# One mixer-and-experts kernel on one core: the last front unit in halves, dense weights loaded in pieces, two loads moved ahead of a store

## The chip, the core and the metric

The kernel runs on one core of a Trainium2 chip. A core has TensorE (PE, matrix products into PSUM), VectorE (DVE), ScalarE (ACT), GpSimd (POOL) and SyncE (SP), whose queue issues all DMAs here; 16 DMA engines carry them. Each engine runs its own list of instructions in order and waits on semaphores. The metric is the time of one execution in microseconds (us).

## The reference, cut to what matters

Batch B = 4, length L = 1024. A selective state-space layer over `ctx`, gated by the layer norm of `x`, then a dense layer with 8 low-rank experts, top 2 of them per token:

```python
x = einsum('ed,bld->bel', in_proj_w, ctx)             # 1024 channels from 512
u = silu(causal_conv4(x) + conv_b)                    # taps t, t-1, t-2, t-3
dt_lo, Bm, Cm = split(einsum('ke,bel->bkl', x_proj_w, u))   # 32, 16, 16 rows
delta = softplus(dt_proj_w @ dt_lo + dt_proj_b)
state = state * exp(delta * A) + (delta * u) * Bm     # 16 states a channel, over l
y = (sum_n state_n * Cm_n + D * u) * silu(layernorm(x))
x = x + y
x = x + layernorm(x) @ W_base.T + b_base + top2_experts(layernorm(x))
```

## The kernel before, in words

**Tiling.** Channels lie on the 128 partitions and time along the free dimension. A *unit* U = 8 b + c is 128 channels (c = 0 to 7) of batch b. There are 32 *blocks* E, one for each unit's scan, with 16 *steps* each, one for each state n. Step m of block E on VectorE is `scan` (L1055) over 128x1024 elements. The term that it adds is `du * B_n`: for 10 or 11 of the steps VectorE makes it (`drive`, L1040) from a row of B that TensorE spread over the partitions into PSUM (`spread`, L483). For the steps in `B_ROWS` (1, 3, 6, 8, 11, 14) GpSimd makes it (`drive_rows`, L1187) from `b_rows`, which a DMA spreads. GpSimd multiplies each scan's result with `c_rows` (`product`, L1194), and TensorE adds the 16 products up in `y_ps` (`add_up`, L489). `gated_y` (L1062) makes `yy` of it on VectorE at step 2 of the next block.

**Front.** Before block E can run, its batch needs projection, convolution, SiLU (this gives `u`, stored to `u_d`), and the reduction by `w_x`, which gives `xd`: the 16 B rows, the 16 C rows and the 32 `dt` rows. For batches 1 to 3 this lies between the steps of earlier blocks. For batch 0 it stands alone ahead of block 0: for c = 0 to 7 TensorE projects into `row[c % 2]` (`project_first`), ScalarE begins the convolution (`begin_first`), VectorE adds three taps (`taps_first`), ScalarE applies SiLU (`finish_u`), TensorE reduces into `y_ps` (`reduce_first`). Then ScalarE copies `xd` in two halves (`take_xd`), VectorE splits it into three bf16 parts in six instructions, and TensorE makes `dt` (L590) and the first spread.

**SP's queue.** It stores each `u` and loads the next projection weights; after the last unit it loads the context of batch 1, `skip` (u of unit 0 read back, which GpSimd multiplies with `delta` to `du` in `make_du`), stores the B and C rows to `bc_d`, and, when that has landed, loads `b_rows` and `c_rows` from it. Of `c_rows` there is a ring of 4 places: the load for product q waits for product q - 4. Then follow the dense layer's weights `w_ra` (288 KB) and `w_o` (4 MB); the dense layer starts in block 9.

**Blocks 9 to 31** hold the dense layer for one tile of 128 tokens each beside the scans, and the tiles that are left run after the last scan.

Of the kernel before, what the change touches and what calls it, by code (L numbers as in the profile page):

```python
# [88 lines left out]
def program(nc, t_in, out):  # L89
# [5 lines left out]
    with ExitStack() as stack:  # L95
# [77 lines left out]
        first_begun, first_step, first_done, conv_first = (sem(n) for n in ("first_begun", "first_step", "first_done", "conv_first"))  # L173
        split_high, split_rest, split_mid, split_rest2, split_done = (sem(n) for n in (
# [44 lines left out]
        def _(sp):  # L219
# [110 lines left out]
            for c in range(NE):  # L330
                load_w_in(c + 2)
                store_u(c)
            for k in range(NK):
                load_ctx(1, k)
            load_u_again(0)
# [8 lines left out]
            sp.dma_start(w_ra[:, :, :], t_in["w_ra"]).then_inc(dense_in, 16)  # L344
            sp.dma_start(w_o[:, :, :], t_in["w_o"]).then_inc(dense_in, 16)

            def section(E, m):
# [3 lines left out]
                if last:  # L351
                    if m == 4:
                        store_bc(b + 1)
                    for i, n in enumerate(B_ROWS):
                        if m == max(n + 1, 6 + i):
                            load_b(b + 1, i)
                if m == 2 and j >= 1:
                    store_half(j - 1, 1)
# [53 lines left out]
        def _(pe):  # L412
# [157 lines left out]

            def reduce_first(c):

                pe.wait_ge(u_ready, c + 1)
                for h in range(2):
                    last = nc.tensor.matmul(y_ps[:, half(h)], w_x[:, c, :], decay[:, c % DECAYS, half(h)], start=(c == 0), stop=(c == NE - 1),
                                            skip_group_check=True)
                last.then_inc(u_used, 1)
# [4 lines left out]
            for c in range(2, NE):  # L582
                project_first(c)
                reduce_first(c - 2)
            reduce_first(NE - 2)
            reduce_first(NE - 1)
# [9 lines left out]
            def section(E, m):  # L596
# [19 lines left out]
                if dense and m == 4:  # L616
                    if j == 0:
                        pe.wait_ge(dense_in, 32)
# [57 lines left out]
        def _(act):  # L676
# [51 lines left out]
            def soften(E):  # L728
# [4 lines left out]
                else:  # L733
                    act.wait_ge(dt_ready, 2)
                    nc.scalar.activation(delta[:, 0, :], row[0][:, :], ACT.Softplus, bias=ch[:, 0, NC + 1:NC + 2]).then_inc(delta_ready, 1)
# [27 lines left out]
            def take_xd(b, h):  # L763

                if b == 0:
                    act.wait_ge(u_used, NE)
# [114 lines left out]

            table(LOGEXP)
# [11 lines left out]
            for c in range(NE):  # L894
# [3 lines left out]
                if c == 1:  # L898
                    gate_rows(0)
            table(SOFT)  # L900
# [101 lines left out]
        def _(dve):  # L1002
# [13 lines left out]

            def taps(E, i):
# [87 lines left out]
            for c in range(NE):  # L1105
                taps_first(c)

# [174 lines left out]
```

## Time and profile before

| | us |
|---|---|
| median of 3 runs (lowest, highest) | 2097.69 (2096.14, 2099.48) |
| profiled execution, its own time | 2104.84 |
| its span | 2103.0 |

| engine | busy us | share of the span |
|---|---|---|
| TensorE (PE) | 1782.0 | 85% |
| VectorE (DVE) | 1787.7 | 85% |
| GpSimd (POOL) | 1767.9 | 84% |
| ScalarE (ACT) | 1256.7 | 60% |

The profile is of one execution. Its rows give for an instruction, or a run of like ones, the start and duration, the engine, the line of the kernel, the operation, and its output and inputs. In brackets stands the idle time of the engine just before it, with what ended it.
### The profile page before, as it was taken

Reading aid. Unit: us, or ns where it says so; the run is one execution under the profiler, and the core shown is the slowest. Engines: PE = TensorE matmul, PEld = TensorE weight load, DVE = VectorE, ACT = ScalarE, POOL = GpSimd, SP = SyncE. Lnnn points to the kernel's source line nnn. Section 1 sums busy time; section 2 is a strip of 40 time slices with the busy share of each in tenths; the row PEclk is TensorE's granted clock in tenths of the full one; section 3 lists DMA queues with packets and bytes.
Section 4 is the critical chain, followed back from the end, with each engine's and each line's share of the span. In section 5 each row is a group of like instructions: output and inputs, shape, how many; then the busy total and the mean of one; then the engine's idle time right before and its main releaser. Section 6 shows DMA issues by size and latency. Waiting matters only on the chain.

```text
span 2103.0 us, 23735 instructions
## 1 busy us (share of the span) xinstructions
PE 1782.0 (85%) x7996; PEld 1094.4 (52%) x7996; DVE 1787.7 (85%) x1432; ACT 1256.7 (60%) x1701; POOL 1767.9 (84%) x796
## 2 busy tenths in 40 slices
PE   8767777877788899889989899899888888888999
PEld 3344554545455555555655555555555555555554
DVE  3589999999899999998989999988989999997111
ACT  3346655555666766766666666766666666663431
POOL 0279999999999999999989999999999999997200
PEclk9788778778779999999989999999999999989999
DMA  4565555576756666697755566686665666565200
GB/s 153 216 251 186 200 198 193 196 244 234 281 197 197 228 217 214 216 320 257 245 194 192 213 217 210 207 310 243 237 206 199 212 200 215 196 214 214 108 30 30
DMA packets 157977, 435.88 MB, mean 207 GB/s; under 512 B 14528, under 2 KB 47552, under 8 KB 157728
## 3 DMA queue, kind: packets, MB, share of 16 engines
q1 hardware_dynamic: 157856, 434.37, 60.2%
q8 instruction: 63, 1.03, 0.2%
q14 instruction: 58, 0.48, 0.1%
HBM read 383.46 MB, written 50.86 MB: 207 GB/s over the span
## 4 chain that ended last, share of the span: by engine, by line
DVE 39%; PE 29%; issue 17%; POOL 7%; ACT 5%; DMA 3%; DVEq 0%; SPq 0%; POOLq 0%; ACTq 0%
DVE state L1055 23%; DVE row L1040 10%; PE bank_a L545 8%; PE y_ps L489 6%; POOL prod L1194 5%; DVE conv L1032 3%; PE bank_b L545 3%; PE row L567 3%; PE row L483 2%; PE bank_b L449 2%; PE bank_a L556 1%; ACT decay L809 1%; PE bank_b L440 1%; POOL drive_rows L1187 1%; DMA xrow<-in_x 1%
## 5 line engine op out<-in xcount | busy, mean ns | idle before, releaser
L1194 POOL TENSOR_TENSOR prod<-state,c_rows 128x1024 f32<-128x1024 f32 x512 | 1200.3, 2359 | 91.8 <-DVE state L1055 40.3
L1055 DVE TENSOR_TENSOR_SCAN state<-decay,row 128x1024 f32<-128x1024 f32 x334 | 762.8, 2284 | 7.4
L489 PEld LDWEIGHTS y_ps<-ident,prod 128*128 128x128 f32 x4096 | 520.2, 152 | 296.2 <-issue 189.8
L489 PE MATMUL y_ps<-ident,prod 128*128 128x128 f32 x4096 | 592.5, 294 | 44.2 <-POOL prod L1194 41.2
L1040 DVE TENSOR_TENSOR row<-du,row 128x1024 f32<-128x1024 f32 x334 | 404.3, 1210 | 41.6 <-PE row L483 37.7
L809 ACT ACTIVATE row<-delta,a 128x1024 f32<-128x1024 f32 x178 | 199.0, 1118 | 379.9 <-DVE state L1055 379.0
L1187 POOL TENSOR_TENSOR drive_rows<-du,b_rows 128x1024 f32<-128x1024 f32 x178 | 420.9, 2365 | 1.9 <-DMA b_rows<-bc_d 1.9
L1055 DVE TENSOR_TENSOR_SCAN state<-row,drive_rows 128x1024 f32<-128x1024 f32 x178 | 404.7, 2274 | 17.9 <-POOL drive_rows L1187 16.8
L545 PE MATMUL bank_a<-w_o,xnT 128*128 128x512 f32 x816 | 402.0, 625 | 18.1 <-DVE x L1102 18.1
L809 ACT ACTIVATE decay<-delta,a 128x1024 f32<-128x1024 f32 x334 | 374.1, 1135 | 0.0
L483 PE MATMUL row<-parts,sel 96*128 96x512 bf16 x668 | 223.6, 419 | 173.9 <-DVE state L1055 171.6
L545 PEld LDWEIGHTS bank_a<-w_o,xnT 128*128 128x128 f32 x816 | 158.2, 201 | 168.6 <-issue 134.2
L483 PEld LDWEIGHTS row<-parts,sel 96*128 96x128 bf16 x668 | 56.6, 103 | 213.1 <-DVE state L1055 204.3
L1177 POOL TENSOR_TENSOR du<-delta,skip 128x1024 f32<-128x1024 f32 x32 | 75.4, 2356 | 88.5 <-DMA skip<-u_d 88.5
L440 PE MATMUL bank_b<-ctx,w_in 128*128 128x512 f32 x288 | 137.5, 609 | 0.0
L678 ACT ACT_TABLE_LOAD x97 | 124.5, 1283 | 2.4 <-PEq L1273 0.7
L685 ACT ACTIVATE xrow<-xrow 128x1024 f32<-128x1024 f32 x32 | 33.7, 1053 | 114.9 <-DMA xrow<-in_x 114.9
L459 PE MATMUL bank_b<-ident,xrow 128*128 128x128 f32 x256 | 48.3, 320 | 46.0 <-ACT delta L725 40.7
L449 PE MATMUL bank_b<-xd,w_bdt 32*128 32x512 f32 x124 | 86.6, 784 | 0.0
L556 PE MATMUL bank_a<-w_bdt,gT 65*128 65x512 f32 x110 | 63.2, 658 | 25.2 <-ACT gT L870 25.2
L1032 DVE SCALAR_TENSOR_TENSOR conv<-bank_b,ch,conv 128x512 f32<-128x512 f32 (+3 forms) x108 | 80.9, 749 | 3.3
L440 PEld LDWEIGHTS bank_b<-ctx,w_in 128*128 128x128 f32 x288 | 54.4, 196 | 50.8 <-issue 47.4
(131 smaller groups left out, 1636.8 us busy)
## 6 DMA issues: line engine op xcount, KB each, us to landing
c_rows<-bc_d SPq DMA_DIRECT2D x512, 512.0 KB, 4.4
xrow<-in_x SPq DMA_DIRECT2D x32, 512.0 KB, 7.1
skip<-u_d SPq DMA_DIRECT2D x32, 512.0 KB, 6.0
yy_d<-yy SPq DMA_DIRECT2D x32, 512.0 KB, 6.3
b_rows<-bc_d SPq DMA_DIRECT2D x24, 512.0 KB, 8.5
u_d<-conv SPq DMA_DIRECT2D x24, 512.0 KB, 5.3
ctx<-u_d SPq DMA_DIRECT2D x48, 256.0 KB, 5.8
x<-in_x SPq DMA_DIRECT2D x24, 512.0 KB, 5.9
```

The source lines that it names most:

```text
L440: last = nc.tensor.matmul(bank[:, :], w_in[:, U % 2, k, :], ctx[:, k, half(h)], start=(k == 0), stop=(k == NK - 1))
L449: nc.tensor.matmul(bank_b[:, :], w_bdt[96:96 + DR, E % NE * P:(E % NE + 1) * P], xd[96:96 + DR, half(h)], start=True, stop=True).then_inc( ...
L483: last = nc.tensor.matmul(row[n % 2][:, half(h)], sel[:, SPREAD.index(n), :], parts[:, E // NE % 2, half(h)], start=True, stop=True)
L489: last = nc.tensor.matmul(y_ps[:, i * P:(i + 1) * P], source[:, i * P:(i + 1) * P], ident[:, :], start=(first and i % (H // P) == 0), stop ...
L545: nc.tensor.matmul(at.sums[h][:, :], at.xnT[:, k, :], w_o[:, k, half(h)], start=(k == 0), stop=False)
L678: nc.scalar.preload_act_table_set(name)
L809: nc.scalar.activation(to[:, :], delta[:, E % 2, :], ACT.Exp, scale=a[:, E % NE, n:n + 1]).then_inc(decay_ready, 1)
L1032: nc.vector.scalar_tensor_tensor(to, bank[:, 0:end - h * H - back], ch[:, c, NC - 1 - back:NC - back], to, ALU.mult, ALU.add).then_inc(con ...
L1040: nc.vector.tensor_tensor(row[n % 2][:, :], du[:, E % 2, :], row[n % 2][:, :], ALU.mult).then_inc(dve_drive, 1)
L1055: nc.vector.tensor_tensor_scan(state[:, q % STATES, :], factor, term, 0.0, ALU.mult, ALU.add).then_inc(scan_done, 1)
L1187: nc.gpsimd.tensor_tensor(drive_rows[:, i % DRIVES, :], du[:, E % 2, :], b_rows[:, k, :], ALU.mult).then_inc(pool_drive, 1)
L1194: nc.gpsimd.tensor_tensor(prod[:, q % PRODS, :], state[:, q % STATES, :], c_rows[:, q % RING, :], ALU.mult).then_inc(prod_ready, 1)
```

## The change

Three things are changed.

*The last unit of batch 0's front (c = 7) runs in two halves of 512 columns.* `project_end` does all four k of half 0, then those of half 1, with a semaphore after each. `begin_end`, `taps_end`, `finish_end` and `reduce_end` work on a half each. `take_xd` of half 0 waits for half 0's reduction alone. The softplus of block 0 (`soften`) is in halves too, each behind its half of `dt`.

*The dense weights are loaded during block 1*: `w_ra` at step 0, and `w_o` in eight pieces of 512 KB at steps 3 to 10.

*`skip` for block 0 and the context of batch 1 are issued before the store of the last u.*

On TensorE, around the last unit (L567/L572/L583 projections, L575/L601/L594 reductions, L590/L620 `dt`), before:

```order
L567 MATMUL row<-ctx,w_in 128x512 x8
L575 MATMUL y_ps<-decay,w_x 128x512 x2
L567 MATMUL row<-ctx,w_in 128x512 x8
L575 MATMUL y_ps<-decay,w_x 128x512 x6
L590 MATMUL row<-xd,w_bdt 128x512 x2
L483 MATMUL row<-parts,sel 128x512 x2
```

and the same place in the change:

```order
L601 MATMUL y_ps<-decay,w_x 128x512 x2
L583 MATMUL row<-ctx,w_in 128x512 x8
L601 MATMUL y_ps<-decay,w_x 128x512 x4
L594 MATMUL y_ps<-decay,w_x 128x512 x2
L620 MATMUL row<-xd,w_bdt 128x512 x2
L488 MATMUL row<-parts,sel 128x512 x2
```

The count is the same; L583 goes half by half, and the last unit's two reductions are now L594, with a wait each.

On SP's queue, from the store of unit 6 to the loads of `b_rows` and the dense weights, before (L245 stores u, L226 context, L261 `skip`, L266 `bc_d`):

```order
L245 DMA u_d<-decay 128x1024
L235 DMA w_in<-in_w_in 128x512
L245 DMA u_d<-decay 128x1024
L226 DMA ctx<-in_ctx 128x1024 x4
L261 DMA skip<-u_d 128x1024
L266 DMA bc_d<-xd 32x1024
L282 DMA b_rows<-bc_d 128x1024
L275 DMA c_rows<-bc_d 128x1024
L282 DMA b_rows<-bc_d 128x1024
L275 DMA c_rows<-bc_d 128x1024 x2
L282 DMA b_rows<-bc_d 128x1024 x4
L344 DMA w_ra<-in_w_ra 128x576
L345 DMA w_o<-in_w_o 128x8192
```

and in the change:

```order
L247 DMA u_d<-decay 128x1024
L237 DMA w_in<-in_w_in 128x512
L263 DMA skip<-u_d 128x1024
L228 DMA ctx<-in_ctx 128x1024 x4
L247 DMA u_d<-decay 128x1024
L268 DMA bc_d<-xd 32x1024
L284 DMA b_rows<-bc_d 128x1024
L277 DMA c_rows<-bc_d 128x1024
L284 DMA b_rows<-bc_d 128x1024
L277 DMA c_rows<-bc_d 128x1024 x2
L284 DMA b_rows<-bc_d 128x1024 x4
L277 DMA c_rows<-bc_d 128x1024 x6
```

`skip` and the context stand ahead of the last u store, and `c_rows` follows `b_rows` directly.

On SP's queue in block 1, from step 0 on, in the change (L359 and L361 are the dense weights, L290 stores `yy`, L242 loads `xrow`):

```order
L359 DMA w_ra<-in_w_ra 128x576
L277 DMA c_rows<-bc_d 128x1024 x3
L361 DMA w_o<-in_w_o 128x1024
L290 DMA yy_d<-yy 128x8x128
L277 DMA c_rows<-bc_d 128x1024
L361 DMA w_o<-in_w_o 128x1024
L277 DMA c_rows<-bc_d 128x1024
L361 DMA w_o<-in_w_o 128x1024
L242 DMA xrow<-in_x 128x1024
L277 DMA c_rows<-bc_d 128x1024
L361 DMA w_o<-in_w_o 128x1024
```

One piece stands behind each `c_rows`; three more pairs like this follow, and `skip` and `w_in` between them.

```diff
--- before.py
+++ after.py
@@ -171,6 +171,8 @@
         x0_ready, x_ready, conv_begun, conv_step, conv_done, u_ready, u_used, us_used, xd_copied = (sem(n) for n in (
             "x0_ready", "x_ready", "conv_begun", "conv_step", "conv_done", "u_ready", "u_used", "us_used", "xd_copied"))
         first_begun, first_step, first_done, conv_first = (sem(n) for n in ("first_begun", "first_step", "first_done", "conv_first"))
+        end_begun, end_step, end_done, end_x, end_u, end_used = (sem(n) for n in (
+            "end_begun", "end_step", "end_done", "end_x", "end_u", "end_used"))
         split_high, split_rest, split_mid, split_rest2, split_done = (sem(n) for n in (
             "split_high", "split_rest", "split_mid", "split_rest2", "split_done"))
         first_split = sem("first_split")
@@ -329,10 +331,11 @@
             sp.dma_start(sel[:, :, :], t_in["pick"]).then_inc(sel_in, 16)
             for c in range(NE):
                 load_w_in(c + 2)
+                if c == NE - 1:
+                    load_u_again(0)
+                    for k in range(NK):
+                        load_ctx(1, k)
                 store_u(c)
-            for k in range(NK):
-                load_ctx(1, k)
-            load_u_again(0)
             store_bc(0)
             load_b(0, 0)
             load_c(0)
@@ -341,8 +344,6 @@
                 load_c(i)
             for i in range(2, len(B_ROWS)):
                 load_b(0, i)
-            sp.dma_start(w_ra[:, :, :], t_in["w_ra"]).then_inc(dense_in, 16)
-            sp.dma_start(w_o[:, :, :], t_in["w_o"]).then_inc(dense_in, 16)
 
             def section(E, m):
                 b, r, j = E // NE, E % NE, E - LATE
@@ -354,6 +355,10 @@
                     for i, n in enumerate(B_ROWS):
                         if m == max(n + 1, 6 + i):
                             load_b(b + 1, i)
+                if E == 1 and m == 0:
+                    sp.dma_start(w_ra[:, :, :], t_in["w_ra"]).then_inc(dense_in, 16)
+                if E == 1 and m in range(3, 3 + NE):
+                    sp.dma_start(w_o[:, m - 3, :], t_in["w_o"][:, m - 3, :]).then_inc(dense_in, 16)
                 if m == 2 and j >= 1:
                     store_half(j - 1, 1)
                 if m == 3:
@@ -568,11 +573,32 @@
                                                 start=(k == 0), stop=(k == NK - 1), skip_group_check=True)
                 last.then_inc(x0_ready, 1)
 
+            def project_end():
+
+                c = NE - 1
+                pe.wait_ge(first_done, c - 1)
+                pe.wait_ge(w_in_in[c % 2], 16 * (c // 2 + 1))
+                for h in range(2):
+                    for k in range(NK):
+                        last = nc.tensor.matmul(row[c % 2][:, half(h)], w_in[:, c % 2, k, :], ctx[:, k, half(h)],
+                                                start=(k == 0), stop=(k == NK - 1), skip_group_check=True)
+                    last.then_inc(x0_ready if h else end_x, 1)
+
+            def reduce_end(h):
+
+                c = NE - 1
+                if h == 0:
+                    pe.wait_ge(end_u, 1)
+                else:
+                    pe.wait_ge(u_ready, NE)
+                nc.tensor.matmul(y_ps[:, half(h)], w_x[:, c, :], decay[:, c % DECAYS, half(h)], start=False, stop=True,
+                                 skip_group_check=True).then_inc(u_used if h else end_used, 1)
+
             def reduce_first(c):
 
                 pe.wait_ge(u_ready, c + 1)
                 for h in range(2):
-                    last = nc.tensor.matmul(y_ps[:, half(h)], w_x[:, c, :], decay[:, c % DECAYS, half(h)], start=(c == 0), stop=(c == NE - 1),
+                    last = nc.tensor.matmul(y_ps[:, half(h)], w_x[:, c, :], decay[:, c % DECAYS, half(h)], start=(c == 0), stop=False,
                                             skip_group_check=True)
                 last.then_inc(u_used, 1)
 
@@ -580,10 +606,14 @@
             project_first(1)
             pe.wait_ge(w_x_in, 16)
             for c in range(2, NE):
-                project_first(c)
+                if c < NE - 1:
+                    project_first(c)
+                else:
+                    project_end()
                 reduce_first(c - 2)
             reduce_first(NE - 2)
-            reduce_first(NE - 1)
+            reduce_end(0)
+            reduce_end(1)
             pe.wait_ge(w_bdt_in, 16)
             for h in range(2):
                 pe.wait_ge(xd_copied, h + 1)
@@ -615,7 +645,7 @@
                     turn(j, m - 2, beside, True)
                 if dense and m == 4:
                     if j == 0:
-                        pe.wait_ge(dense_in, 32)
+                        pe.wait_ge(dense_in, 16 * (NE + 1))
                     route(j, beside)
 
                 for i, at in enumerate(front_plan(E)[0]):
@@ -731,8 +761,10 @@
                     act.wait_ge(v_copied, 2 * E)
                     nc.scalar.activation(delta[:, E % 2, :], delta[:, E % 2, :], ACT.Softplus).then_inc(delta_ready, 1)
                 else:
-                    act.wait_ge(dt_ready, 2)
-                    nc.scalar.activation(delta[:, 0, :], row[0][:, :], ACT.Softplus, bias=ch[:, 0, NC + 1:NC + 2]).then_inc(delta_ready, 1)
+                    for h in range(2):
+                        act.wait_ge(dt_ready, h + 1)
+                        last = nc.scalar.activation(delta[:, 0, half(h)], row[0][:, half(h)], ACT.Softplus, bias=ch[:, 0, NC + 1:NC + 2])
+                    last.then_inc(delta_ready, 1)
 
 
             def begin_conv(E, i):
@@ -763,7 +795,10 @@
             def take_xd(b, h):
 
                 if b == 0:
-                    act.wait_ge(u_used, NE)
+                    if h == 0:
+                        act.wait_ge(end_used, 1)
+                    else:
+                        act.wait_ge(u_used, NE)
                 else:
                     act.wait_ge(us_used, ((b - 1) * 2 + h + 1) * NE)
                     act.wait_ge(dt_ready, 2 * NE * b)
@@ -879,6 +914,24 @@
                 nc.scalar.activation(decay[:, c % DECAYS, :], row[c % 2][:, :], ACT.Identity, bias=ch[:, c, NC:NC + 1],
                                      scale=ch[:, c, NC - 1:NC]).then_inc(first_begun, 1)
 
+            def begin_end(h):
+
+                c = NE - 1
+                if h == 0:
+                    act.wait_ge(end_x, 1)
+                    act.wait_ge(u_used, c - DECAYS + 1)
+                    act.wait_ge(u_out[c % 2], 16 * ((c - DECAYS) // 2 + 1))
+                else:
+                    act.wait_ge(x0_ready, NE)
+                nc.scalar.activation(decay[:, c % DECAYS, half(h)], row[c % 2][:, half(h)], ACT.Identity, bias=ch[:, c, NC:NC + 1],
+                                     scale=ch[:, c, NC - 1:NC]).then_inc(end_begun, 1)
+
+            def finish_end(h):
+
+                act.wait_ge(end_done, h + 1)
+                u = decay[:, (NE - 1) % DECAYS, half(h)]
+                nc.scalar.activation(u, u, ACT.Silu).then_inc(u_ready if h else end_u, 1)
+
             table(LOGEXP)
             act.wait_ge(consts_set, 2)
             act.wait_ge(ch_in, 16)
@@ -891,12 +944,16 @@
             act.wait_ge(a_step, 1)
             nc.scalar.activation(a[:, :, 0:DS], a[:, :, 0:DS], ACT.Copy, scale=-1.0).then_inc(a_step, 1)
             table(SILU)
-            for c in range(NE):
+            for c in range(NE - 1):
                 if c:
                     begin_first(c)
                 finish_u(c)
                 if c == 1:
                     gate_rows(0)
+            for h in range(2):
+                begin_end(h)
+            for h in range(2):
+                finish_end(h)
             table(SOFT)
             for h in range(2):
                 take_xd(0, h)
@@ -1014,6 +1071,18 @@
                     nc.vector.scalar_tensor_tensor(decay[:, c % DECAYS, back:], row[c % 2][:, 0:L - back], ch[:, c, NC - 1 - back:NC - back],
                                                    decay[:, c % DECAYS, back:], ALU.mult, ALU.add).then_inc(first_step if back < NC - 1 else first_done, 1)
 
+            def taps_end(h):
+
+                c = NE - 1
+                dve.wait_ge(end_begun, h + 1)
+                for back in range(1, NC):
+                    if back > 1:
+                        dve.wait_ge(end_step, h * (NC - 2) + back - 1)
+                    first = H if h else back
+                    to = decay[:, c % DECAYS, first:half(h).stop]
+                    nc.vector.scalar_tensor_tensor(to, row[c % 2][:, first - back:half(h).stop - back], ch[:, c, NC - 1 - back:NC - back],
+                                                   to, ALU.mult, ALU.add).then_inc(end_step if back < NC - 1 else end_done, 1)
+
             def taps(E, i):
 
                 U, h = HALVES[E][i]
@@ -1102,8 +1171,10 @@
                 nc.vector.tensor_tensor(x, x, at.sums[h][:, :], ALU.add).then_inc(res_ready, 1)
 
             dve.wait_ge(ch_in, 16)
-            for c in range(NE):
+            for c in range(NE - 1):
                 taps_first(c)
+            for h in range(2):
+                taps_end(h)
 
 
             rest = state[0:96, 0, :]
```

## Rows read from the trace of the kernel before

**Rows 1.** Busy time by stretch: from:to, us, each engine's busy us, granted clock, DMA share, GB/s.

```profile
91.40:165.80 74.40, 49.76 (x197) 29.10 (x197) 60.93 (x41) 37.91 (x47) 59.93 (x26) 0.73 0.72 268
165.80:223.00 57.20, 42.78 (x192) 26.60 (x192) 54.98 (x38) 32.95 (x40) 53.59 (x24) 0.80 0.58 195
```

**Rows 2.** Timeline of VectorE: start, us, operation, idle before and releaser.

```profile
106.14 1.23 DVE L1040 TENSOR_TENSOR row<-du,row 128x1024 f32<-128x1024 f32 x1 [2.64 <-PE row L483]
...
122.02 2.29 DVE L1055 TENSOR_TENSOR_SCAN state<-row,drive_rows 128x1024 f32<-128x1024 f32 x1 [6.67 <-POOL drive_rows L1187]
...
128.96 2.29 DVE L1055 TENSOR_TENSOR_SCAN state<-row,drive_rows 128x1024 f32<-128x1024 f32 x1 [1.20 <-POOL drive_rows L1187]
...
165.75 1.22 DVE L1062 TENSOR_TENSOR yy<-gate,y_ps 128x1024 f32<-128x1024 f32 x1 [1.73 <-PE y_ps L489]
...
223.03 1.22 DVE L1062 TENSOR_TENSOR yy<-gate,y_ps 128x1024 f32<-128x1024 f32 x1 [1.73 <-PE y_ps L489]
```

**Rows 3.** Timeline of GpSimd, its fourth product.

```profile
117.35 2.34 POOL L1194 TENSOR_TENSOR prod<-state,c_rows 128x1024 f32<-128x1024 f32 x1 [12.55 <-DMA c_rows<-bc_d]
```

**Rows 4.** DMA issues: count, KB each, us to landing; b_rows: minimum, median, maximum.

```profile
w_o<-in_w_o SPq DMA_DIRECT2D x1, 4096.0 KB, 21.7
...
bc_d<-xd SPq DMA_DIRECT2D x1, 128.0 KB, 6.5
...
c_rows<-bc_d SPq DMA_DIRECT2D x1, 512.0 KB, 22.5
...
DMA to landing us min/median/max: 3.9/9.1/11.1
```

**Rows 5.** Timeline around the last unit of the front.

```profile
68.61 1.06 ACT L760 ACTIVATE decay<-decay 128x1024 f32<-128x1024 f32 x1 [3.98 <-DVE decay L1014]
...
71.80 3.60 PE L575 MATMUL y_ps<-decay,w_x 128*128 128x512 f32 x8
...
73.24 3.92 DVE L1014 SCALAR_TENSOR_TENSOR decay<-row,ch,decay 128x1023 f32<-128x1023 f32 x3 [4.67 <-ACT decay L879]
...
77.19 1.06 ACT L760 ACTIVATE decay<-decay 128x1024 f32<-128x1024 f32 x1 [3.98 <-DVE decay L1014]
...
78.30 3.19 PE L575 MATMUL y_ps<-decay,w_x 128*128 128x512 f32 x4 [2.90 <-ACT decay L760]
...
81.53 1.08 ACT L773 ACTIVATE xd<-y_ps 128x512 f32<-128x512 f32 x2 [1.98 <-PE y_ps L575]
...
86.06 1.11 ACT L735 ACTIVATE delta<-row,ch 128x1024 f32<-128x1024 f32 x1 [3.44 <-PE row L590]
```

**Rows 6.** Timeline at the start of block 0.

```profile
88.15 1.01 PE L483 MATMUL row<-parts,sel 96*128 96x512 bf16 x2 [2.13 <-DVE parts L1118]
...
88.98 2.35 POOL L1177 TENSOR_TENSOR du<-delta,skip 128x1024 f32<-128x1024 f32 x1 [88.54 <-DMA skip<-u_d]
...
91.36 1.23 DVE L1040 TENSOR_TENSOR row<-du,row 128x1024 f32<-128x1024 f32 x1 [3.36 <-POOL du L1177]
...
95.59 2.29 DVE L1055 TENSOR_TENSOR_SCAN state<-row,drive_rows 128x1024 f32<-128x1024 f32 x1 [0.67 <-POOL drive_rows L1187]
```

**Rows 7.** Groups by line and shape, 60 to 170 us: busy us, mean ns | idle before.

```profile
L1032 DVE SCALAR_TENSOR_TENSOR conv<-bank_a,ch,conv 128x512 f32<-128x512 f32 x6 | 4.5, 746 | 0.1
...
L750 ACT ACTIVATE conv<-bank_a,ch 128x512 f32<-128x512 f32 x2 | 1.5, 759 | 0.0
```

**Rows 8.** Timeline of SP's queue: issue of the DMAs.

```profile
72.00 0.33 SPq L235 DMA_DIRECT2D w_in<-in_w_in  x1
...
78.27 0.33 SPq L245 DMA_DIRECT2D u_d<-decay  x1
...
82.64 0.32 SPq L266 DMA_DIRECT2D bc_d<-xd  x1
```

**Rows 9.** Landings of c_rows issued from 150 to 215 us.

```profile
DMA to landing us min/median/max: 3.5/4.3/5.6
```

**Rows 10.** Busy time by stretch, columns as in rows 1.

```profile
94.80:106.00 11.20, 8.31 (x21) 4.22 (x22) 8.00 (x5) 4.40 (x5) 9.99 (x5) 0.50 1.05 398
```

## The prediction, as it was written before the changed kernel had run

> **What bounds the kernel now.** I read the page first, then the engines by stretch, then VectorE's timeline for its idle times, then GpSimd's timeline and the DMA landings for what ended them, and last the timeline from 64 to 96 us. In the steady part VectorE sets the pace: in block 1 (166 to 223 us) it is busy 54.98 of 57.20 us, GpSimd 53.59 [rows 1], and one block takes 57.28 us from one `yy` product to the next (165.75 to 223.03) [rows 2]. Neither has time to win back a loss, so what the start loses stays lost. Block 0 with its lead-in (91.4 to 165.8) is longer: VectorE is busy 60.93 of 74.40 us [rows 1]. Its idle pieces are 2.64 us behind a spread on TensorE, 6.67 and 1.20 us behind GpSimd's drive rows, and the 1.73 us before `yy` that block 1 has as well [rows 2]. GpSimd was late because its fourth product sat 12.55 us waiting for its `c_rows` [rows 3]. That load took 22.5 us to land where its like in block 1 takes 4.3; the DMA issued just ahead of it is `w_o`, 4 MB, 21.7 us [rows 4, 9]. Before block 0 lies a serial chain through the last unit (c = 7) of the front: projection, taps, SiLU, reduction, `xd`, the split, `bc_d`, `b_rows`, first drive row [rows 5, 6].
>
> **Part 1, the dense weights out of block 0.** This removes 4.3 MB from the queue between the six `b_rows` and the fourth `c_rows`. The 12.55 us wait goes, and I ask what is late next. The slowest `b_rows` needs 11.1 us [rows 4], and the last is issued at 93.3, so the queue ahead of the fourth `c_rows` is drained at 104.4. Another 0.5 MB at the 398 GB/s of that stretch [rows 10] is 1.3 us: it lands at 105.7. GpSimd is ready for it at 104.8 (117.35 less 12.55) [rows 3], so 0.9 us of wait is left. VectorE wants the drive row behind that product only after its convolution at 115.4 (122.02 less 6.67) [rows 2]. With product and drive row at 2.35 us each the drive row is ready at 105.7 + 4.7 = 110.4, 5 us early. The next one (for the scan that starts at 128.96 now) follows product 5, which can start when scan 5 ends at 113.1, and is ready at 113.1 + 4.7 = 117.8; VectorE wants it at 128.96 - 6.67 - 1.20 = 121.1. So both waits go: 6.67 + 1.20 = 7.9 us gained. Bounds: 5 if a third of it comes back as a late `c_rows`, and 7.9 + 2.6 = 10.5 if the wait behind TensorE goes too. That wait is a matter of the clock: from 94.8 to 106 the granted clock is 0.50 [rows 10], the 1.2 GHz level, and TensorE does a gate turn, a projection piece, an add-up and the spread one after the other. The cause, pauses of TensorE before, is still there, so I keep the 2.6 us of wait.
>
> The Trainium skill (TensorE: Matmul & The Clock Gate, "What's actually happening") says that the throttled clock is the default and activity releases it. The trace agrees in that TensorE falls to 0.50 after its 2.90 us pause before the last reduction [rows 5, 10]. By this rule a front with a shorter pause could keep 2.4 GHz for the matmuls behind it; my sum does not count on it.
>
> **Part 2, the dense weights into block 1.** Added there: `w_ra` (0.3 MB) at step 0 and eight 0.5 MB pieces of `w_o` at steps 3 to 10, one behind each `c_rows` on SP's queue; also queued there are `yy_d` at step 3, `xrow` at 5, `skip` and `w_in` at 7. 4.2 MB over eight steps of 57.28 / 16 = 3.6 us is 146 GB/s on top of 195 [rows 1], 341 together, under the 398 that the queue has done [rows 10]. A piece puts off its successor by 1.3 us. A `c_rows` is issued three products before its use, some 10 us, and lands in 4.3 (5.6 at most) [rows 9], so 4 us are spare. `xrow` may come 1.3 us late, and ScalarE has its idle pieces there. I take 0.3 us of loss, bounds 0 and 3. The 9-fold count that TensorE waits for before its first routing (block 9) has been reached for hundreds of us. SP issues ten DMAs where it issued two; each takes 0.3 to 0.5 us of a 3.6 us step, hidden in its waits for products.
>
> **Part 3, the last unit in halves.** Half 0 of the projection is done at 71.8 - 8 x 0.43 = 68.5 (0.43 is 3.60 us / 8 matmuls, rounded down for the overlap of the last). ScalarE is free at 69.7 [rows 5], and starts half 0 then. A half takes 0.76 on ScalarE, and 3 x 0.75 on VectorE [rows 7], where 1.20 and 3.92 stood for the whole. So: half 0 begun 69.7 to 70.5, taps to 72.8; half 1 begun 72.0 to 72.8 (the projection ends at 71.97), taps to 75.1; SiLU of half 1 to 75.7 (1.06 for a whole, 0.55 taken for a half), against 78.25. TensorE works at unit 5's and 6's reductions up to 75.4, then half 0's to 76.3 and half 1's to 77.2, at 0.43 a matmul since it no longer pauses. The table load (1.28, from 75.7) ends at 77.0, so the `xd` copies run 77.0 to 78.1 in place of 81.53 to 82.61 [rows 5]. Gain up to here 4.5 us. Extra work is 0.3 us on ScalarE and 0.6 on VectorE, counted in. From the end of `xd` to the spread are 88.15 - 82.61 = 5.54 us of splitting on VectorE, and the spread takes 1.0 [rows 6]: the first drive on VectorE can start at 84.7 instead of 91.36, and its scan ends at 84.7 + 1.24 + 2.29 = 88.2.
>
> **Part 4, u's first load and the context ahead of u's last store.** Today GpSimd's first product waits for `skip` until 88.98, though `delta` is ready at 87.2 [rows 5, 6]. Now `skip` is issued at 72.4 behind `w_in`, first in line, and is there long before `delta`: with softplus in halves `delta` is ready at 80.0 with the fast clock, 81.7 with the slow. `du` then ends by 84.1 at the latest, before the spread at 84.7, so it no longer decides. The next thing that does is the first drive row: `bc_d` is stored, lands, `b_rows` is loaded (3.9 us), GpSimd multiplies (2.35). Between 78.27 and 82.64 SP queued u 0.52, context 2.10, `skip` 0.52 and `bc_d` 0.13 MB, 3.27 together, and `bc_d` landed at 89.2, 6.5 us after its issue [rows 8, 4]: 10.9 us after the first issue. Now 3.54 MB (`w_in` is 0.26) are queued from 72.0 on; in proportion 11.8 us, so 83.8. Hence `b_rows` at 87.7, the drive row at 90.05, scan 1 at 90.1 where it now starts at 95.59 [rows 6]: **5.5 us gained**. If `bc_d` takes its 6.5 us again (78.15 + 6.5 = 84.7), it is 4.6. If it lands by 81.9, scan 0's end at 88.2 decides, and it is 7.4. I stay near the middle, since the proportion uses the same transfers. The last u store lands with that queue, at 83; only the third decay factor waits for it, made at 83.5 or later.
>
> The Trainium skill (DMA: Bandwidth & Descriptors, "Anatomy of one DMA") gives a fixed cost of about 2 us for one DMA, whatever its size. The 6.5 us of the 128 KB `bc_d` [rows 4] is over three times that, so here the queue ahead decides. By the rule's price `bc_d` would land near 80.4 and the front would gain 7.4 us; the total would be 15.0 instead of 13.1.
>
> **The sum.** 5.5 + 7.9 - 0.3 = 13.1 us. The profiled execution took 2104.84 us (span 2102.98), so it would take 2091.7. It lies 7.15 above the median of 2097.69; I take the same difference off the median: **2084.6 us**. Behind block 1 the order of all engines is unchanged; only the phase of the granted clock moves, for which I allow 2 us each way.
>
> **Rivals.**
> - *More than the sum.* TensorE's 2.6 us wait in block 0 goes as well, or `bc_d` is early (+1.9). For it: shorter pauses in the front. Against: the pause of the split remains. 2097.7 - 13.1 - 2.6 = 2082, with both 2080.
> - *The front gives little.* The context loads, now in front of the u store, hold `bc_d` up, and halves cost more than in the rows: gain 3 instead of 5.5, or less. For it: `bc_d` today lands only when the queue is empty. Against: this queue begins 6.3 us earlier. 2087 to 2090.
> - *The stall stays.* The six `b_rows` and not `w_o` held up `c_rows`. Then only the front's gain shows: 2092. Against: 104.4 is when the last `b_rows` lands, 12.9 us before the product starts.
> - *Slower than before.* In block 1 the pieces of `w_o`, with `yy_d`, `xrow` and `skip`, make each `c_rows` late, and GpSimd, with 3.6 us of idle in the block, passes on every wait. The spare is 4 us; for the change to come out slower by over 0.2% it would need 13.4 + 4.2 = 17.6 us of waits, 2.2 at each of eight products beyond the spare, so landings from some 12 us on where 4.3 are seen. The price from there: 2102. Against: 341 of 398 GB/s.
>
> **Chances.** Forecast 0.66; more than the sum 0.15; front gives little 0.10; the stall stays 0.05; slower 0.02; the rest, a drift of the clock's phase that gives back all, 0.02. 0.2% (4.2 us) is about what a measurement of this kernel can tell from no change, so faster begins below 2093.5: all of the first three and most of the fourth, 0.94; same 0.04; slower 0.02. For the range I take the forecast with its bounds, 2080 for the upper case, and up to 2090 for the front that gives little.
>
> **What would show it.** `xd` copied near 78.1, first scan near 86, second near 90; `skip` no longer GpSimd's releaser; no `c_rows` wait over 2 us in block 0, and the first `yy` at 165.75 - 13.4 = 152.4; block 1 at 57.3 to 57.6. A first `yy` later than 156, or a second one more than 60 us behind it, would make the prediction wrong.

## The result, and the profile after

| | before | changed |
|---|---|---|
| median of 13 runs, us (lowest to highest) | 2096.65 (2093.27 to 2100.5) | 2086.44 (2078.69 to 2093.05) |
| ratio, 95% interval | | 0.9948 (0.9934 to 0.9961) |
| profiled execution / span, us | 2104.84 / 2103.0 | 2086.44 / 2084.7 |

The change takes 10.9 us off by the ratio (8.2 to 13.8; the medians lie 10.2 apart), where 13.1 had been forecast; the median is 2086.44, forecast 2084.6. Every ratio here is against the kernel before as it ran beside that kernel, and of fast executions alone, which leaves out one of e9's eleven, at 3634.83 us. Two later sets of runs of the same kernel gave 0.9925 (0.9907 to 0.9944) and 0.9951 (0.9933 to 0.9968). The profiled execution of before took 4.3 us more than the longest of its 13 timed ones, so the 18.3 us between the two spans (2103.0 less 2084.7) overstate the gain.

VectorE's timeline of the changed kernel (start, us, operation, idle before) answers to [rows 2, 6]:

```profile
79.98 3.43 DVE L1189 CAST parts<-state 32x1024 bf16<-32x1024 f32 x2
...
86.65 1.23 DVE L1109 TENSOR_TENSOR row<-du,row 128x1024 f32<-128x1024 f32 x1 [1.27 <-PE row L488]
...
90.61 2.29 DVE L1124 TENSOR_TENSOR_SCAN state<-row,drive_rows 128x1024 f32<-128x1024 f32 x1 [0.41 <-POOL drive_rows L1258]
...
100.40 1.23 DVE L1109 TENSOR_TENSOR row<-du,row 128x1024 f32<-128x1024 f32 x1 [1.88 <-PE row L488]
...
151.94 1.22 DVE L1131 TENSOR_TENSOR yy<-gate,y_ps 128x1024 f32<-128x1024 f32 x1 [1.72 <-PE y_ps L494]
209.22 1.22 DVE L1131 TENSOR_TENSOR yy<-gate,y_ps 128x1024 f32<-128x1024 f32 x1 [1.72 <-PE y_ps L494]
```

Scan 1 starts at 90.61 instead of 95.59, and the first `yy` at 151.94 instead of 165.75: 13.8 us are won by then. (0.2 of them are not the change's: the front, up to where nothing was edited, ran that much earlier in this execution; see the column "unit 6" below.) No scan in block 0 waits for drive rows after scan 1. Block 1, with the dense weights in it, takes 57.28 us as before.

The wait behind TensorE is 1.88 us where it was 2.64. TensorE no longer pauses 2.90 us before the last reduction, and its granted clock (the figure behind the five engines' busy times) is low for a shorter time: 0.50 from 79 to 106 us before, and now

```profile
82.50:99.00 16.50, 9.29 (x17) 3.36 (x18) 14.21 (x9) 8.47 (x10) 11.13 (x6) 0.50 0.90 328
99.50:116.00 16.50, 13.43 (x77) 9.14 (x76) 15.42 (x11) 7.67 (x11) 14.93 (x8) 1.00 0.64 225
```

GpSimd's timeline has the fourth product's wait [rows 3] down to

```profile
88.24 2.34 POOL L1258 TENSOR_TENSOR drive_rows<-du,b_rows 128x1024 f32<-128x1024 f32 x1 [5.37 <-DMA b_rows<-bc_d]
...
100.36 2.36 POOL L1265 TENSOR_TENSOR prod<-state,c_rows 128x1024 f32<-128x1024 f32 x1 [0.54 <-DMA c_rows<-bc_d]
```

and the front's chain on ScalarE and SP's queue reads

```profile
69.33 0.76 ACT L926 ACTIVATE decay<-row,ch 128x512 f32<-128x512 f32 x1
71.77 0.78 ACT L926 ACTIVATE decay<-row,ch 128x512 f32<-128x512 f32 x1 [1.67 <-PE row L583]
...
74.94 0.63 ACT L933 ACTIVATE decay<-decay 128x512 f32<-128x512 f32 x1 [1.82 <-DVE decay L1083]
...
76.88 1.08 ACT L808 ACTIVATE xd<-y_ps 128x512 f32<-128x512 f32 x2
```

```profile
77.99 0.32 SPq L268 DMA_DIRECT2D bc_d<-xd  x1
83.89 0.32 SPq L284 DMA_DIRECT2D b_rows<-bc_d  x1
```

`xd` is copied by 77.96 (forecast 78.1), and `bc_d` has landed when SP issues the first `b_rows` at 83.89 (forecast 83.8).

One row says less than I had counted on. The landings of `c_rows` issued in block 1 (152 to 209 us), 3.5/4.3/5.6 before [rows 9], are now

```profile
DMA to landing us min/median/max: 3.4/5.2/9.4
```

The slowest is up 3.8 us, where I had 1.3. No product of GpSimd waits for `c_rows` in block 1, but the tightest one, issued at 175.10, lands 9.2 us later and 1.9 us before its product starts at 186.16; in block 1 of before the tightest had 5.5 us. The pieces are hidden, by a small margin.

### The profile page after: what moved, and what is told of

Its sections match the earlier page's. It is cut to its first block, busy times and chain, and to the rows that moved or that the text cites. A ratio compares the mean times of both kernels' runs of the same rounds, so it can differ in the third digit from the quotient of the medians.

```text
span 2084.7 us, 23748 instructions
## 1 busy us (share of the span) xinstructions
PE 1768.3 (85%) x7996; PEld 1086.3 (52%) x7996; DVE 1789.8 (86%) x1435; ACT 1259.4 (60%) x1704; POOL 1768.5 (85%) x796
## 4 chain that ended last, share of the span: by engine, by line
DVE 39%; PE 29%; issue 16%; ACT 6%; POOL 5%; DMA 4%; DVEq 0%; SPq 0%; POOLq 0%; ACTq 0%
DVE state L1124 24%; DVE row L1109 11%; PE bank_a L550 8%; PE y_ps L494 5%; POOL prod L1265 4%; DVE conv L1101 3%; PE bank_b L550 3%; PE row L572 2%; DMA xrow<-in_x 2%; PE row L488 2%; ACT decay L844 2%; PE bank_a L561 2%; PE bank_b L454 1%; PE bank_b L445 1%; ACT L708 1%
```

## The experiments

Each is an edit of the kernel before or of the changed one. "First yy" is the start of the first `yy` product, "tail" the span behind the last one. "Unit 6" is the end of unit 6's SiLU on ScalarE, the last one that no edit touches. It falls anywhere from 67.88 to 69.67 us, and its place goes into every time behind it, so the column "won" gives how much earlier than in before the first yy stands when counted from there. Two kernels with the same front and weights in the same place (before and e6) still differ by 0.4 in it. e6 and e11 were traced and not timed further.

| run | time ratio (95%) | unit 6 | scan 1 | first yy | won | last yy | tail |
|---|---|---|---|---|---|---|---|
| before | | 69.67 | 95.59 | 165.75 | | 1933.32 | 169.7 |
| e1 dense only | 0.9969 (0.9952 to 0.9986) | 68.90 | 95.00 | 157.00 | 8.0 | 1925.38 | 172.0 |
| e2 front only | 0.9975 (0.9957 to 0.9992) | 68.90 | 91.69 | 161.89 | 3.1 | 1931.88 | 169.7 |
| e3 halves only | 0.9994 (0.9978 to 1.0011) | 67.88 | 91.20 | 161.21 | 2.8 | 1930.67 | 169.8 |
| e4 order only | 0.9981 (0.9966 to 0.9997) | 68.91 | 94.08 | 160.19 | 4.8 | 1925.85 | 169.8 |
| changed | 0.9948 (0.9934 to 0.9961) | 69.43 | 90.61 | 151.94 | 13.6 | 1912.65 | 172.0 |
| e8 changed again | 0.9925 (0.9907 to 0.9944) | 69.54 | 91.29 | 152.49 | 13.1 | 1912.65 | 172.1 |
| e12 changed, third | 0.9951 (0.9933 to 0.9968) | 68.73 | 90.36 | 152.45 | 12.4 | 1919.90 | 170.4 |
| e5 du late | 0.9919 (0.9895 to 0.9943) | 69.24 | 90.88 | 151.84 | 13.5 | 1908.93 | 172.0 |
| e6 pieces in place | | 69.12 | 95.54 | 165.65 | -0.4 | 1931.64 | 170.2 |
| e7 context later | 0.9916 (0.9895 to 0.9937) | 68.72 | 88.63 | 150.32 | 14.5 | 1908.26 | 171.9 |
| e9 four pieces | 0.9941 (0.9922 to 0.996) | 69.11 | 91.20 | 152.07 | 13.1 | 1912.22 | 169.75 |
| e10 e7 and e9 | 0.9937 (0.9913 to 0.996) | 69.06 | 88.97 | 150.84 | 14.3 | 1910.95 | 169.8 |
| e11 more pieces | | 69.54 | 91.03 | 152.35 | 13.3 | 1912.88 | 169.65 |

**e1, the dense weights alone.** In block 1's step function, with the two lines ahead of block 0 taken out (`w_ra` goes to step 0 likewise, not shown):

```diff
+                if E == 1 and m in range(3, 3 + NE):
+                    sp.dma_start(w_o[:, m - 3, :], t_in["w_o"][:, m - 3, :]).then_inc(dense_in, 16)
```

> The kernel before with the dense weights alone moved into block 1; front and queue order as before. My theory (the 4.3 MB ahead of c_rows made the 12.55 us wait, VectorE lost 6.67 + 1.20 us by it): the wait of the fourth product is under 2 us, first scan stays at 92.6, first yy at 165.75 - 7.9 = 157.9, block 1 at 57.3 us, the time 7.9 us (0.38%) below before. Rival (the six b_rows held c_rows up): the wait stays over 10 us, first yy near 165. Rival (the pieces cost as much in block 1): the second yy is over 60 us behind the first.

First yy at 157.00, 8.75 us earlier, of which 0.77 is the run's earlier front: 8.0 are won. Block 1 is 57.28 us. No wait for `c_rows` is left in GpSimd's waits from 80 to 160 us:

```profile
POOL du L1179 <- DMA skip<-u_d: 87.5, 1, 87.5
POOL prod L1196 <- DVE state L1057: 3.7, 3, 2.1
POOL drive_rows L1189 <- DMA b_rows<-bc_d: 2.3, 1, 2.3
POOL prod L1196 <- PE y_ps L491: 0.6, 1, 0.6
```

The 7.9 us of part 1 hold. The rival "the six `b_rows` did it" falls.

**e2, e3, e4, the front's parts.** e2 is the changed kernel with the weights put back; e3 has the old queue order besides; e4 is the kernel before with this alone:

```diff
                 load_w_in(c + 2)
+                if c == NE - 1:
+                    load_u_again(0)
+                    for k in range(NK):
+                        load_ctx(1, k)
                 store_u(c)
```

> The changed kernel with the dense weights put back ahead of block 0's c_rows: halves and queue order changed. Theory (the parts add up): scan 1 at 90.6 as in the changed kernel (95.59 before), the whole wait for c_rows is back (12 to 13 us), first yy at 165.75 - 5 to - 6 = 160 to 161, the time 5 us (0.24%) below before. Rival (the wait for c_rows is set by the clock time at which the weights have landed and swallows the front's gain): first yy at 165 or later, no gain.

> The kernel before with the last unit in halves alone: SP's queue order and dense weights as before. Theory (bc_d lands when the queue ahead of it has drained; that queue now begins with the last u store, 2.7 us earlier): xd copied at 78.0, but skip is issued near 78.3 and lands near 86.3, so du and the first scan wait for it (du near 86.4 to 88.7, first scan near 90), bc_d lands at 86.5, scan 1 at 92.9, a gain of 2.7 us and not of 4.5. Rival (xd decides): scan 1 at 91.1, a gain of 4.5.

> The kernel before with only the queue order changed (skip and context ahead of the last u store). Theory: xd stays at 82.6; skip and context have landed by then, only the u store (0.5 MB) is ahead of bc_d, which lands near 85.7 instead of 89.2; du starts at 87.2 when delta is there, no longer at 88.98; scan 1 near 93.0, a gain of 2.5 us. The casts of the split take 0.70 us each, since GpSimd's du starts only behind them. Rival (queue order changes nothing, bc_d always takes 6.5 us): scan 1 at 95.6.

Counted from unit 6, scan 1 is 2.6 us early in e3 (2.7 expected; the 4.4 between the bare starts would have passed for its rival, and the time of e3 can't be told from before's), 0.7 in e4 (2.5 expected; e5 below shows why) and 3.1 in e2 (5 expected), against 4.2 to 4.7 in the three traces of the changed kernel. The first yy of e4 is won by 4.8 us, more than e2's 3.1 with both parts, where 5 to 6 had been expected. What fits all five traces with the weights ahead of `c_rows` (e6 is below) is one fixed distance: from the landing of `bc_d` to the start of the fourth product.

| | bc_d landed by (first b_rows issued) | fourth product starts | difference |
|---|---|---|---|
| before | 89.20 | 117.35 | 28.15 |
| e6 | 88.68 | 117.23 | 28.55 |
| e2 | 85.30 | 113.46 | 28.16 |
| e3 | 84.67 | 112.80 | 28.13 |
| e4 | 84.00 | 111.77 | 27.77 |

From that product to the first yy it is 48.4 us in each. So with the weights there, only `bc_d`'s landing counts, and the front's other gains are swallowed. That e2 won less than e4 is because `bc_d` took 7.8 us in it; the changed kernel, with the same queue up to there, shows 5.9, 6.6 and 6.3. What made it longer in e2 was not tried. In e4 `bc_d` is issued at 81.84 into a queue that has little left, and takes

```profile
bc_d<-xd SPq DMA_DIRECT2D x1, 128.0 KB, 2.1
```

while in the changed kernel, issued 3.9 us earlier, it sits behind the context:

```profile
bc_d<-xd SPq DMA_DIRECT2D x1, 128.0 KB, 5.9
```

Both have landed by 84.0. The halves bring `xd` forward, and most of it is lost again in this queue; order and halves overlap, they don't add.

The Trainium skill (DMA: Bandwidth & Descriptors, "Anatomy of one DMA") gives a fixed cost of about 2 us for one DMA. The section is on DMAs issued from GpSimd, and these are SP's, but the 2.1 us of e4 agrees with it. The rest of the 5.9 and 6.5 us is the queue ahead, as e7 shows below.

**e5, the first du behind the split.**

```diff
                 pool.wait_ge(delta_ready, E + 1)
+                if E == 0:
+                    pool.wait_ge(first_split, FIRST_SPLITS)
```

> The changed kernel, but GpSimd makes the first du only when VectorE has finished the split of xd (it waits for the six split instructions). Theory (the two 32-row casts took 1.7 us each instead of 0.70 because GpSimd's product ran beside them): they take 0.70 us again, the split ends at 83.4 instead of 85.4, du runs 83.4 to 85.8, the first drive starts near 85.8 instead of 86.65; but b_rows lands as before (GpSimd's drive row at 88.24), so scan 1 stays at 90.6 and the time is unchanged within 0.1%. Rival (the casts are slow for another reason, such as the DMA traffic or their place): they stay at 1.7 us.

VectorE's timeline has the casts back at 0.70 each, against 3.43 for two in the changed kernel:

```profile
79.79 1.40 DVE L1189 CAST parts<-state 32x1024 bf16<-32x1024 f32 x2
...
85.69 1.23 DVE L1109 TENSOR_TENSOR row<-du,row 128x1024 f32<-128x1024 f32 x1 [2.52 <-POOL du L1250]
...
90.88 2.29 DVE L1124 TENSOR_TENSOR_SCAN state<-row,drive_rows 128x1024 f32<-128x1024 f32 x1 [1.64 <-POOL drive_rows L1260]
```

and scan 1 is where it was. As expected. e4 has the same collision, by chance: `du` starts at 86.45, 0.07 us before the last cast of the split, which takes 2.83 us for 0.68:

```profile
86.52 2.83 DVE L1119 CAST parts<-state 32x1024 bf16<-32x1024 f32 x1
```

In both the cast ends 0.5 to 0.6 us after GpSimd's product does (83.41 after 82.87 in the changed kernel, 89.35 after 88.79 in e4), so it stood for nearly all of the product. That is against what I expected of e4 (`du` behind the casts), and with the 2.15 us more in the split it is why scan 1 won so little there. The time ratio of e5 is 0.9919 (0.9895 to 0.9943); e8, on the same chip, 0.9925.

**e6, w_o in pieces at the old place** (eight DMAs where one stood).

> The kernel before with w_o loaded in eight 512 KB DMAs instead of one, at the old place. Theory (what counts is the number of bytes ahead of c_rows in the queue): the fourth product still waits about 12.5 us, a little more for seven further issues of 0.45 us each that stand before the fourth c_rows on SP, first yy at 165.8 to 168. Rival (one 4 MB DMA blocks the queue as a whole, pieces let c_rows in between): the wait falls under 5 us.

The fourth product waits 12.49 us. Bytes count here, not how many DMAs carry them.

**e7, the context behind the first rows** (e5, and `load_ctx(1, k)` moved behind `load_c(0)`).

> The changed kernel with the late du of e5 and the context of batch 1 loaded behind the first b_rows and c_rows. Theory (the context, 2.1 MB, is what bc_d waits behind): bc_d, issued at 78.0, lands by 81 instead of 83.9, the first b_rows by 85, so scan 1 follows scan 0 at once, near 89.3 instead of 90.6; first yy at 151.94 - 1.3 = 150.6. The context is there before TensorE's first projection of batch 1 near 95.5. The time is 1.3 us (0.06%) below the changed kernel, which the clock cannot resolve; the trace can. Rival: the second b_rows is now late and the product or the drive row behind it gives the gain back (scan 3 waits).

`bc_d`, issued at 77.28, has landed at 79.22:

```profile
77.28 0.32 SPq L268 DMA_DIRECT2D bc_d<-xd  x1
79.22 0.32 SPq L284 DMA_DIRECT2D b_rows<-bc_d  x1
79.58 0.43 SPq L277 DMA_DIRECT2D c_rows<-bc_d  x1
80.06 2.29 SPq L228 DMA_DIRECT2D ctx<-in_ctx  x4
```

`bc_d` takes 1.9 us with the context out of its way. Scan 1 follows scan 0 at 88.63, first yy at 150.32: 1.5 us before e5's, of which 0.5 is the run's earlier front. The ratio is 0.9916 (0.9895 to 0.9937), not to be told from e5 and e8.

**e8, the changed kernel again.**

> The changed kernel once more, for a second trace and more times. Theory (13.8 us are won up to the first yy, and what is missing from that in the medians, 3 us of 13.8, is lost by the way TensorE's granted clock falls over the later blocks, which differs from run to run): the first yy again at 151.9 within 0.3 us, the blocks up to 8 the same within 1 us each, and the difference of the two traces, up to several us, in blocks 9 to 31 and the tail. Rival (the loss is a fixed wait that the change caused): the same wait at the same place in both traces.

The first yy is 0.55 us behind that of the first trace, not within 0.3, and between the second yy and the last the two agree within 0.6 us, so what is missing was not lost there. The rival has it, in the tail. The tail is 172 us in the changed kernel, e1, e5, e7 and e8, and 169.7 to 169.8 in before, e2, e3 and e4. In the DMA view from the last yy on, the last `yy_d` store has an extra packet beside it in the changed kernel, of the queue that the profile labels as instructions (first two rows of queues, then the landing):

```profile
q1 hardware_dynamic: 1040, 0.52, 34.0%
q14 instruction: 1, 0.01, 0.4%
...
yy_d<-yy SPq DMA_DIRECT2D x1, 512.0 KB, 3.7
```

Before, over the same store, there is q1 alone:

```profile
q1 hardware_dynamic: 1040, 0.52, 38.3%
...
yy_d<-yy SPq DMA_DIRECT2D x1, 512.0 KB, 3.2
```

The queue of instructions brings 8 KB: its packet starts 3.8 us after the last yy, while the store's last packets move (2.1 to 4.1 us after it, in before). In before the packet came after 10.2. It is SP's list that moves it: e1 and e6, which lengthen that list alone, have it at 3.7 and 3.8, and e2 and e3, whose other engines' lists are changed and SP's is not longer, at 10.1 and 10.3. GpSimd's first addition of the tail, which waits for the loads behind that store, starts 0.6 us late; TensorE pauses longer, and its granted clock falls once to 1.2 GHz (second row: 0.66 over 4 us; here stretch, busy us by engine, clock, DMA share, GB/s):

```profile
1923.65:1929.65 6.00, 4.49 (x16) 2.12 (x15) 0.69 (x1) 5.08 (x11) 6.00 (x6) 0.94 1.03 415
1929.65:1933.65 4.00, 4.00 (x8) 1.74 (x7) 0.00 (x0) 0.71 (x2) 4.00 (x5) 0.66 1.02 400
```

**e9 to e12, where the fetch falls.** e9 is the changed kernel with

```diff
-                if E == 1 and m in range(3, 3 + NE):
-                    sp.dma_start(w_o[:, m - 3, :], ...
+                if E == 1 and m in (3, 5, 7, 9):
+                    sp.dma_start(w_o[:, m - 3:m - 1, :], ...
```

e10 is e7 with the same, e11 the changed kernel with `w_ra` in eight pieces.

> The changed kernel with w_o in four 1 MB pieces (steps 3, 5, 7, 9 of block 1) instead of eight. In the traces so far the last yy_d store lands in 3.7 us in all six kernels with w_o in pieces (an 8 KB instruction packet of q14 falls into it, 4 us after the last yy), in 3.2 us in the four with w_o in one DMA (that packet comes 10 us after it), and the tail behind the last yy is 171.9 to 172.1 or 169.6 to 169.9 us. Theory (SP's list is seven DMAs longer, so its instructions are fetched earlier and the fetch hits the store; TensorE then pauses longer and its clock falls once): with only three more, the packet comes 7 to 9 us after the last yy, the store lands in 3.2, the tail is 169.7, the time 2.3 us below the changed kernel's. c_rows still has 4 us to spare in block 1 (a piece holds it up 2.6 us), so block 1 stays at 57.3. Rival (the tail is longer for where w_o lies in time or for its piece size): tail 172 again.

> e7 (first du behind the split, context behind the first b_rows and c_rows) with w_o in four pieces. Theory: first yy near 150.4 as in e7 and tail 169.7, so 1.5 + 2.3 = 3.8 us (0.18%) below the changed kernel; the fastest so far, 16 to 19 us below before. Rival: as in e9, tail 172.

> The changed kernel with w_ra in eight pieces too, seven further DMAs on SP in block 1. Theory (the place of the instruction fetch decides, not the pieces): the q14 packet comes another 6 us earlier, ahead of the last yy_d store, which then lands in 3.2 us; tail 169.7. Rival (more and smaller pieces make the tail longer): tail 172 or more.

> The changed kernel a third time, as the reference for e9 to e11 on the same chip. First yy at 151.9 to 152.5, the q14 packet 4 us after the last yy, the last store landing in 3.7 us, tail 172.0; median 2085 to 2087. What differs from the other two traces lies between the second yy and the last.

The packet's place is its start.

| | SP's DMAs against before | instruction packet after last yy | last store lands in | tail |
|---|---|---|---|---|
| before | 0 | 10.2 | 3.2 | 169.7 |
| e9 | +3 | 8.2 | 3.2 | 169.75 |
| changed | +7 | 3.8 | 3.7 | 172.0 |
| e11 | +14 | -18.1 | 3.2 | 169.65 |

e11, with the most and smallest pieces, has the short tail, so it is the place of the fetch and not the pieces. Its packet moved by 22 us and not by the 6 expected, so the count of DMAs alone does not give the place. The same two stretches in e9, from its last yy on, keep the full clock:

```profile
1923.20:1929.20 6.00, 5.07 (x18) 2.27 (x17) 0.69 (x1) 5.09 (x12) 6.00 (x6) 1.00 1.03 419
1929.20:1933.20 4.00, 4.00 (x23) 2.75 (x22) 0.02 (x1) 0.27 (x2) 4.00 (x4) 1.00 1.04 412
```

e6 and e12 show the two steps apart: the store lands late in both (3.7), but the clock fell in neither, and the tails are 170.2 and 170.4. e12 is the changed kernel itself, where 172.0 had been expected, so that one kernel shows either.

In e9 block 1 is 57.70 us, 0.4 longer, against what was expected. No product waits for `c_rows` in it. It is `xrow` that comes later, 8.4 us after its issue behind the second 1 MB piece (7.2 in the changed kernel, 4.8 in before). ScalarE waits 3.05 us for it (1.82 in the changed kernel), makes its part of the convolution late, and VectorE waits for that:

```profile
174.50 1.06 ACT L715 ACTIVATE xrow<-xrow 128x1024 f32<-128x1024 f32 x1 [3.05 <-DMA xrow<-in_x]
```

```profile
179.74 2.33 DVE L1101 SCALAR_TENSOR_TENSOR conv<-bank_b,ch,conv 128x512 f32<-128x512 f32 x3 [0.32 <-ACT conv L782]
```

The whole times don't resolve any of this: e9 0.9941 (0.9922 to 0.996), e10 0.9937 (0.9913 to 0.996), against e12's 0.9951. e10 has the first yy at 150.84, the tail 169.8 and the lowest time seen (2075.36), but it can't be called faster than the changed kernel; the 3.8 us expected of it are not shown.

## Why the prediction was right, and where a size was off

- **Part 1 (7.9 us): right.** The wait for `c_rows` is 0.54 us (0.9 forecast), both waits of VectorE are gone, and e1 gives the term alone, 8.0.
- **Part 2 (0.3 us): right by the block, too easy in its reason.** Block 1 lost nothing, but `c_rows` took up to 9.4 us, not 7, and the tightest landed 1.9 us ahead of its product, where 4 us were to spare by my sum. `xrow`, which I had 1.3 us late, was 2.4, and 1.2 us more of it cost e9 0.4 us in the block. The dense weights are nine DMAs, not the ten of the prediction, and behind the four pieces of the order shown above the diff stand four more, not three.
- **Part 3 (4.5 us to xd): right to 0.1 us** (4.4 counted from unit 6). Behind it the way from `xd` to the spread took 7.6 us and not 5.5, because two casts ran beside GpSimd's `du`; the first drive is at 86.65, not 84.7. It cost nothing, since the drive row decides scan 1 (90.61; 90.1 forecast). e5 shows it.
- **Part 4: right in its mechanism, a little high in size.** `bc_d` lands behind the queue at 83.9, and `skip` is no longer waited for. That the landing meets the forecast of 83.8 to 0.1 us is partly luck: in the same kernel it was 84.7 in e8 and 83.6 in e12. Counted from unit 6, scan 1 is won by 4.7, 4.2 and 4.3 us in the three traces, for the 5.5 forecast; the 4.6 that the prediction gave for a `bc_d` of 6.5 us is nearer. That parts 3 and 4 overlap (e3 and e4) was not seen.
- **The wait behind TensorE, kept whole at 2.6 us: too high.** It is 1.88, as the low clock ended at 99 us and not at 106: 0.8 us of the rival "more than the sum" came true. It makes up for most of what part 4 lacks. The first yy is won by 12.4 to 13.6 us in the three traces, for 13.4 forecast.
- **The term left out** is "behind block 1 the order of all engines is unchanged": on SP it is not quite, since seven more DMAs move its instruction fetch, and that costs up to 2.3 us in the tail: 0.6 to 0.7 for the store, as in e6 and e12, and some 1.6 more where the clock falls, as in the profiled changed kernel, e8, e1, e5 and e7. The 12.4 to 13.6 won up to the first yy, less 0.7 to 2.3, are 10.1 to 12.9; measured are 10.9 (8.2 to 13.8). How often the clock falls there in executions that were not profiled is not known. The forecast left this term out, and its error of 2.2 us is of that size, but the interval of the measurement is too wide to show that the one is the other.
- **Open:** between the second yy and the last the same kernel took 1703.4, 1702.9 and 1710.2 us in three traces, before 1710.3. The profiled executions with 1710 were also long ones of their kernel (before 8.2 us and e12 4.4 us above the median, the changed kernel at it and e8 1.5 above), so this belongs to the execution more than to the edit. It was not tried what decides it.

## What to carry to other kernels

A small DMA that a chain waits for costs what the queue holds in front of it (1.9 to 2.1 us here with little ahead, 5.9 to 7.8 behind the context): count the bytes issued before it, and issue what nobody needs yet behind it. A bulk load of weights belongs where the loads around it have spare lead, in pieces shorter than that lead, and the lead is to be checked against the slowest landing, not the median, and for every load in that stretch (`xrow` in e9), not only the one that you had in mind. Before a part's gain is read off two traces, line them up at the last place that both have in common: here the front alone moved by up to 1.8 us. When a gain is smaller in the end than at the place where it is made, compare the last stretch of both traces as well: adding instructions to an engine's list moves its fetches.

## What the runs showed of the hardware

- **A cast on VectorE stops while GpSimd multiplies.** 32x1024 fp32 to bf16 takes 0.70 us, and 2.83 or, two together, 3.43 beside a product of GpSimd of 2.34 and 2.49 us; it ends 0.5 to 0.6 us after that product. VectorE's fp32 products of `du` and a row in PSUM were not slowed beside GpSimd's (1.21 us). The Trainium skill has a rule that fits (SBUF — State Buffer, "SBUF: two separate sides"): VectorE's two-port modes and GpSimd share a port pair under an exclusive lock, held for the whole instruction. That the cast runs in such a mode no run here shows.
- **An instruction fetch of 8 KB delays a DMA** that the tail waits for by 0.5 us (3.7 for 3.2), in all seven traces where they coincide.
- **Whole times spread more than their parts**: up to the first yy the changed kernel's traces agree within 0.6 us, its times range over 14 (2078.69 to 2093.05).
